# Field-pair products of six batches a chunk: summed by halving on GpSimd instead of by VectorE, gathers of a duo issued without a pause

## The reference

```python
e = jnp.stack([tbl_0[ids[:, 0]], ..., tbl_39[ids[:, 39]]], axis=1)     # (2048, 40, 64)
p = e[:, rowidx]
q = e[:, colidx]
z = jnp.einsum('bie,fie,bif->bi', p, param, q)                         # (2048, 780)
h = jnp.concatenate([z, dense_ctx], axis=1)
h = jnp.maximum(h @ W_top1 + b_top1, 0.0)                              # 512 wide
h = jnp.maximum(h @ W_top2 + b_top2, 0.0)                              # 256 wide
y = h @ W_top3
```

## Time and profile before

| | us |
|---|---|
| median of three runs | 1375.43 (1375.16 to 1380.41) |
| the profiled execution, its time | 1380.23 |
| its span, first to last instruction | 1378.2 |
| PE busy | 1242.5 |
| DVE busy | 1032.1 |
| POOL busy | 604.4 |
| ACT busy | 697.6 |

### The profile page before, as it was taken

The page is one execution under the profiler, slowest core; times in us unless marked ns, Lnnn a source line. Parts: engine busy times, 40 slices in busy tenths (PEclk is TensorE's granted clock), DMA queues, the critical chain, the costliest instruction groups (busy, mean ns, idle before and its releaser), DMA issues.

```text
span 1378.2 us, 20032 instructions
## 1 busy us (share of the span) xinstructions
PE 1242.5 (90%) x6032; PEld 435.1 (32%) x6032; DVE 1032.1 (75%) x899; ACT 697.6 (51%) x5257; POOL 604.4 (44%) x646
## 2 busy tenths in 40 slices
PE   0446799989899999999999999999999999999999
PEld 0112233233233333333333333333333333333333
DVE  0124687878887878888887878888887888888970
ACT  0013366475554366484555366485555366485441
POOL 4555555555555554555555555554454454000000
PEclk9777899999999999999999999999999999999999
DMA  3111122222222222222222222222222222111100
GB/s 124 26 34 43 49 66 57 65 57 62 60 64 59 65 58 64 57 70 60 58 65 60 63 58 65 58 71 57 56 64 65 53 59 62 41 52 47 47 10 0
DMA packets 50531, 77.55 MB, mean 56 GB/s; under 512 B 14004, under 2 KB 14260, under 8 KB 50296
## 3 DMA queue, kind: packets, MB, share of 16 engines
q1 hardware_dynamic: 29936, 55.26, 13.9%
q0 software_dynamic: 20480, 21.01, 7.9%
q10 hardware_dynamic: 8, 0.01, 0.0%
HBM read 76.22 MB, written 0.01 MB: 55 GB/s over the span
## 4 chain that ended last, share of the span: by engine, by line
PE 68%; DVE 3%; ACT 3%; issue 1%; another core or an unknown queue 0%; DMA 0%; POOL 0%; DVEq 0%
PE ring L476 28%; PE z_ps L495 14%; PE ring L482 12%; PE aux L414 5%; ACT act_prod L327 3%; DVE prod L400 2%; PE aux L446 2%; PE ring L414 2%; PE aux L421 2%; PE ring L477 1%; DVE sums L367 1%; PE aux L428 1%; PE ring L421 0%; DVE dve_prod L400 0%; PE aux L435 0%
## 5 line engine op out<-in xcount | busy, mean ns | idle before, releaser
L400 DVE TENSOR_TENSOR prod<-ring,emb 128x1024 f32<-128x1024 f32 x544 | 636.3, 1218 | 285.9 <-PE ring L477 264.0
L327 ACT ACTIVATE act_prod<-act_prod 128x64 f32<-128x64 f32 x2560 | 611.7, 242 | 144.0 <-DVE act_prod L400 110.6
L282 POOL DMA_INDIRECT stage<-tbl,idx x512 | 482.8, 943 | 450.5 <-issue 242.0
L476 PE MATMUL ring<-emb,raw 64*128 64x512 f32 x1088 | 570.9, 639 | 34.2 <-DVE prod L400 23.2
L477 PE MATMUL ring<-emb,raw 64*128 64x512 f32 x1088 | 571.9, 641 | 0.0
L327 ACT ACTIVATION_READ_ACCUMULATOR act_prod<-act_prod 128x1 f32 x2560 | 482.8, 189 | 2.3 <-issue 2.0
L476 PEld LDWEIGHTS ring<-emb,raw 64*128 64x128 f32 x1088 | 182.3, 192 | 376.9 <-issue 212.7
L495 PE MATMUL z_ps<-prod,sel 128*32 128x512 f32 x2176 | 262.4, 600 | 1.3 <-DVE prod L400 1.3
L482 PE MATMUL ring<-raw,emb 64*128 64x512 f32 x512 | 247.7, 614 | 4.1 <-DVE prod L400 3.1
L483 PE MATMUL ring<-raw,emb 64*128 64x512 f32 x512 | 247.8, 614 | 0.0
L294 ACT ACTIVATE emb<-aux 128x512 f32<-128x512 f32 x80 | 47.4, 592 | 316.4 <-PE aux L446 284.9
(11 more groups left out here) (32 smaller groups left out, 199.3 us busy)
## 6 DMA issues: line engine op xcount, KB each, us to landing
raw<-param_b SPq DMA_DIRECT2D x200, 256.0 KB
stage<-tbl,idx POOLq DMA_INDIRECT x512
kept<-tbl,idx POOLq DMA_INDIRECT x128
W<-W1g SPq DMA_DIRECT2D x1, 1792.0 KB
W<-W2t SPq DMA_DIRECT2D x1, 512.0 KB
idx<-ids_t SPq DMA_DIRECT2D x1, 240.0 KB, 3.6
z<-dense_t SPq DMA_DIRECT2D x4, 32.0 KB, 2.6
idx<-ids_t SPq DMA_DIRECT2D x1, 80.0 KB, 2.0
```

The source lines that it names most:

```text
L282: pool.indirect_dma_start(to[:, t, E * (f % 2) : E * (f % 2) + E], None, tables[f], bass.IndirectOffsetOnAxis(ap=idx[:, c, f, t : t + 1], ...
L327: op = act.activation(part, part, ACT.Copy, accum_out=sums[:, t, at : at + 1])
L400: dve.tensor_tensor(to, ring[:, n % RING, :, :], by, ALU.mult).then_inc(prod_done, 1)
L476: pe.matmul(ring[:, n % RING, 0, :], w[0:E], emb[0:E, PLACE[c, m], :], start=True, stop=True)
```

## The change

DVE no longer sums. Of the same six batches a chunk (now `POOL_SUMS`) POOL halves each unit's 16 runs of 64 five times (32, 16, 8, 4, 2 elements wide) in place and makes the last addition into `sums`: six additions for each unit, each waiting for the one before. These *folds* stand in POOL's program behind the eight gathers of a duo, at most two units behind one duo but for the last place; the table `POOL_AT` says where, by the rule that a unit's fold stands behind the gathers of duo n, the first for which duo n - 2 is turned later than that unit is made. The pause inside a duo is gone. Products for POOL have five places (before: three for DVE); `prod` shrinks from eight to seven, `y_out` becomes a part of `h1`. The first layer of the next chunk waits for the store of `y`, and in the tail ACT waits for the last such store ahead of the turn's copy instead of ahead of `y`.

```diff
-PROD = 2 * BATCH
-DPROD = 3
+PROD = 7
+PPROD = 5
-FLIGHT = 4
+LAG = 2
+FOLDS = 5
...
+POOL_AT = {}
+_order = sorted(DUO_AT)
+_place = 0
+for _c in range(NCH):
+    for _m in POOL_SUMS:
+        for _t in range(BATCH):
+            _u = NU * _c + BATCH * AT["samples", _m] + _t
+            while _place < NCH * DUOS and (
+                _place < LAG or DUO_AT[_order[_place - LAG]] <= _u or len(POOL_AT.get(_place, ())) == 2
+            ):
+                _place += 1
+            POOL_AT.setdefault(_place, []).append((_c, _m, _t))
...
+            def reduce(c, m, t):
+                if c and t == 0:
+                    pool.wait_ge(aux_ready, AUX_NO["turn", c - 1, (m - KEPT) // PER_GROUP] + 1)
+                pool.wait_ge(prod_done, NU * c + BATCH * AT["samples", m] + t + 1)
+                made = sampled(c, m, t)
+                part = pool_prod[:, made % PPROD, :, :].rearrange("p a (j e) -> p (a j) e", e=E)
+                half = E // 2
+                for fold in range(FOLDS):
+                    pool.tensor_tensor(
+                        part[:, :, :half], part[:, :, :half], part[:, :, half : 2 * half], ALU.add
+                    ).then_inc(pool_folded, 1)
+                    pool.wait_ge(pool_folded, FOLDS * made + fold + 1)
+                    half //= 2
+                pool.tensor_tensor(sums[:, t, sums_of(m)], part[:, :, 0], part[:, :, 1], ALU.add).then_inc(pool_reduced, 1)
...
                 for i, (f, t) in enumerate(product((2 * d, 2 * d + 1), range(BT))):
-                    if i == FLIGHT:
-                        pool.wait_ge(landed, 16 * (2 * BT * times + FLIGHT))
-                        pool.sem_inc(pool_waited, 1)
                     pool.indirect_dma_start(
...
+                for x in POOL_AT.get(n, ()):
+                    reduce(*x)
+            for x in POOL_AT.get(NCH * DUOS, ()):
+                reduce(*x)
...
-                if unreduced:
-                    reduce(*unreduced)
-                unreduced = (c, x, t) if kind == "samples" and x in DVE_SUMS else None
...
-                pe.wait_ge(dve_reduced, group_end(c, DVE_SUMS, g))
+                pe.wait_ge(pool_reduced, group_end(c, POOL_SUMS, g))
```

More of the change, by code:

```diff
@@ L43 @@
 NS = DUOS - KEPT
-DVE_SUMS = [KEPT + i for i in (1, 4, 7, 10, 13, 15)]
-ACT_SUMS = [m for m in range(KEPT, DUOS) if m not in DVE_SUMS]
+POOL_SUMS = [KEPT + i for i in (1, 4, 7, 10, 13, 15)]
+ACT_SUMS = [m for m in range(KEPT, DUOS) if m not in POOL_SUMS]
 BATCHES = []
@@ L107 @@
     AUX_AT.setdefault(NU * (_c + 1) + BATCH, []).append(("turn", _c, 1))
-    for _m, _x in zip(DVE_SUMS, [("h1", _c, 0), ("h1", _c, 1), ("h1", _c, 2), ("h1", _c, 3), ("h2", _c, 0), ("h2", _c, 1)]):
+    for _m, _x in zip(POOL_SUMS, [("h1", _c, 0), ("h1", _c, 1), ("h1", _c, 2), ("h1", _c, 3), ("h2", _c, 0), ("h2", _c, 1)]):
         AUX_AT.setdefault(NU * (_c + 1) + BATCH * (AT["samples", _m] + 1), []).append(_x)
@@ L157, in fm_mlp_kernel @@
         act_prod = sb("act_prod", [P, APROD, 2, CH])
-        dve_prod = sb("dve_prod", [P, DPROD, 2, CH])
+        pool_prod = sb("pool_prod", [P, PPROD, 2, CH])
         sums = sb("sums", [P, BT, NS * 2 * ROWS])
@@ L167, in fm_mlp_kernel @@
         h2 = sb("h2", [P, H2 // P, CH])
-        y_out = sb("y_out", [1, CH])
+        y_out = h1[0:1, 0, :]
         ring = ctx.enter_context(nc.psum_tensor("ring", [P, RING, 2, CH], F32))
@@ L186, in fm_mlp_kernel @@
         act_reduced = sem("act_reduced")
-        dve_reduced = sem("dve_reduced")
+        pool_folded = sem("pool_folded")
+        pool_reduced = sem("pool_reduced")
         group_summed = sem("group_summed")
@@ L209, in sampled @@
         def sampled(c, m, t):
-            by = DVE_SUMS if m in DVE_SUMS else ACT_SUMS
+            by = POOL_SUMS if m in POOL_SUMS else ACT_SUMS
             return BT * (len(by) * c + by.index(m)) + t
@@ L301, in save_aux @@
                         act.wait_ge(consts_loaded, 16 * 5)
+                    elif n == 0:
+                        act.wait_ge(stored, 16 * c)
                     act.activation(h1[:, n, :], aux[:], ACT.Relu, bias=b1[:, n : n + 1]).then_inc(aux_saved, 1)
@@ L305, in save_aux @@
                 else:
-                    if c:
-                        act.wait_ge(stored, 16 * c)
-                    act.activation(y_out[:], aux[0:1, :], ACT.Copy).then_inc(aux_saved, 1)
+                    act.activation(y_out, aux[0:1, :], ACT.Copy).then_inc(aux_saved, 1)
                     act.wait_ge(aux_saved, AUX_NO[kind, c, n] + 1)
-                    act.dma_start(out_v[c : c + 1, :], y_out[:]).then_inc(stored, 16)
+                    act.dma_start(out_v[c : c + 1, :], y_out).then_inc(stored, 16)
             def save_z(c, g):
@@ L344, in _ @@
             act.wait_ge(tail_ready, 1)
+            act.wait_ge(stored, 16 * last)
             act.activation(z[:, z_place(last, "samples", 1), :], aux[:], ACT.Copy).then_inc(tail_saved, 1)
@@ L354, in _ @@
             act.wait_ge(tail_ready, 1 + H1 // P + H2 // P + 1)
-            act.wait_ge(stored, 16 * last)
-            act.activation(y_out[:], aux[0:1, :], ACT.Copy).then_inc(tail_saved, 1)
+            act.activation(y_out, aux[0:1, :], ACT.Copy).then_inc(tail_saved, 1)
             act.wait_ge(tail_saved, 1 + H1 // P + H2 // P + 1)
-            act.dma_start(out_v[last : last + 1, :], y_out[:]).then_inc(stored, 16)
+            act.dma_start(out_v[last : last + 1, :], y_out).then_inc(stored, 16)
             act.wait_ge(stored, 16 * NCH)
@@ L362, in _ @@
         def _(dve):
[L363 to L370, removed]
             dve.memset(sel[:], 0.0).then_inc(sel_zero, 1)
@@ L375, in _ @@
             dve.memset(sel[E:P, 31:32], 1.0).then_inc(consts_made, 1)
-            unreduced = None
             for n in range(NCH * NU):
@@ L396, in _ @@
                     else:
-                        if made >= DPROD:
-                            dve.wait_ge(dve_reduced, made - DPROD + 1)
-                        to = dve_prod[:, made % DPROD, :, :]
+                        if made >= PPROD:
+                            dve.wait_ge(pool_reduced, made - PPROD + 1)
+                        to = pool_prod[:, made % PPROD, :, :]
                 dve.tensor_tensor(to, ring[:, n % RING, :, :], by, ALU.mult).then_inc(prod_done, 1)
-                if unreduced:
-                    reduce(*unreduced)
-                unreduced = (c, x, t) if kind == "samples" and x in DVE_SUMS else None
-                if unreduced and t == BT - 1:
-                    reduce(*unreduced)
-                    unreduced = None
         @block.tensor
```

## The result

The changed kernel took 1556.23 us (median of four runs, 1552.49 to 1556.95), the kernel before beside it 1377.33 (four runs, 1375.16 to 1380.41): ratio 1.129 [1.126, 1.132], 12.9% slower. The forecast had the sign, but with 1430 us and an upper end of 1475 it missed the size by 126 us.

What follows compares the result with a forecast made beforehand. It took PE's pace between turns as the bound. POOL's folds delay turns by 21.8 + 1.7 + 3.0 + 11.1 + 4.6 + 12.1 = +54.3 us; on 1380.2 that is 1434.5, less 4.8 gives 1430 us, range 1370 to 1475.

Steps and rivals of the forecast that it cites:

- The folds in POOL's queue: Added work on POOL: gathers wait behind folds and PE's turns wait for folds; +54.3 us in sum.
- turn 0 of chunk 0: PE's first turn, waiting for the folds of place 20: start at 289.7 us instead of 267.9, +21.8.
- to turn 1: Stretch from turn 0 to turn 1 of chunk 0: 157.2 us on POOL, before 155.5, +1.7.
- chunk 1, turn 0 / turn 1: Stretches ending at chunk 1's two turns: 160.4 us (+3.0) and 163.5 us (+11.1), set by POOL.
- chunk 2, turn 0 / turn 1: Stretches ending at chunk 2's two turns: 160.4 us (+4.6) and 163.5 us (+12.1), set by POOL.
- chunk 3, turn 0: Stretch ending at chunk 3's turn 0: POOL needs 150.4 of PE's 159.2 us, so no change.
- F: Price on POOL of one unit's six additions: 3.9 us, between bounds of 2.6 and 4.6; break-even at 2.6.
- the walk: Stepping along POOL's in-order queue of gathers and folds to each turn of PE that waits; +54.3 us in sum.
- The reductions: 96 reductions taken off DVE: hidden behind the layers in chunks 1 to 3 (0), 12 us in chunk 0.
- (b): Pause inside a duo removed from POOL: a duo takes 11.9 us instead of 13.9, 10.0 where folds follow.
- Rival 3: On POOL, eight gathers land later (up to 8 us a stretch) or start late (24), 1500 within reach; chance 0.13, slower.
- R: Rival in the experiments' expectations: folds on POOL cause the loss, by a port or waits, the missing pause is harmless.

Runs made afterwards that it cites:

- m_after: The changed kernel, unchanged, run again on a fifth chip, where the kernel before took 1360.37 us: 1432.49 us.
- g_nopause: The kernel before with only the pause inside a duo taken out, DVE still summing, on a third chip (before: 1377.91): 1538.04 us.
- m_pause_from_12: The kernel before without the pause in duos 0 to 11 of chunk 0 alone, on the fifth chip: 1335.98 us, ratio 0.981 to before.
- e3: The changed kernel with five of each unit's six additions left out (sums not the reference's), on the first follow-up chip (before: 1357.49): 1332.8 us.
- e1: The kernel before with only the pause inside a duo taken out, on the first follow-up chip (before: 1357.49): 1321.74 us.
- m_nopause: The kernel before with only the pause inside a duo taken out, on the fifth chip (before: 1360.37): 1324.78 us.
- e4: The changed kernel, first unit's folds between fourth and fifth gather, second's behind the eighth, old pause in duos without folds: 1516.51 us (before: 1357.49).

## Why the forecast had the sign and not the size

Two mechanisms make the loss, and each was shown by a run that has it alone: the folds by m_after, the missing pause by g_nopause. I forecast the first and left out the second.

**The folds in POOL's queue: right.** On the chip of group 5, where no report is late, the forecast meets the same program:

| us | forecast | measured (m_after) |
|---|---|---|
| turn 0 of chunk 0 | 289.7 | 290.8 |
| to turn 1 | 157.2 | 156.9 |
| chunk 1, turn 0 / turn 1 | 160.4 / 163.5 | 160.3 / 163.8 |
| chunk 2, turn 0 / turn 1 | 160.4 / 163.5 | 160.3 / 163.7 |
| chunk 3, turn 0 | 159.2 | 155.9 |
| time | 1430 | 1432.49 |

The steps hold singly too. The first gathers of duos 9, 10 and 11 in m_after's timeline of POOL:

```profile
113.25 0.94 POOL L310 DMA_INDIRECT stage<-tbl,idx  x1 [2.81 <-issue]
...
125.15 0.94 POOL L310 DMA_INDIRECT stage<-tbl,idx  x1 [2.23 <-issue]
...
142.63 0.95 POOL L310 DMA_INDIRECT stage<-tbl,idx  x1 [0.54 <-issue]
```

A duo without folds takes 11.9 us, as forecast, and duo 10, the first with folds, starts at 125.15 (forecast 123). With folds a duo takes 17.5 us, forecast 17.8. The six turns wait 39.3, 21.2, 4.4, 12.7, 4.4 and 12.5 us for POOL: long at the first and some 10 us at turn 1 of chunks 1 and 2, as written down. Agreement to 3 us has luck in it. F is 0.3 us smaller than forecast, which by the walk (12F to the first turn) alone would have brought turn 0 some 4 us sooner, and duo 10 starts 2 us late. With F = 3.6 the same walk gives 154.8, 159.2 and 161.1 us for stretches that measured 156.9, 160.3 and 163.8. F is also made up otherwise: 3.24 us of work and 0.3 of hand-over, where I had 2.7 and 1.2, so POOL was busy 915 us and not 860. The forecast is also set against a before of 1380, while this chip runs before in 1360: the loss here is 72 us, forecast 54. POOL's queue sets the changed kernel's time; before, which PE sets, is 20 us quicker there. Late reports are the likely reason. In the five stretches from turn 1 of chunk 0 to turn 0 of chunk 3 m_pause_from_12, on the chip of group 5, pauses as before does; they take 756 us there and 776 in before, where 16 of the 17 late products lie in them, 19 us in sum.

**The reductions: right.** Hidden in chunks 1 to 3, 11.0 us in chunk 0, shown by e3 against e1.

**Two slips in the sums.** I took the last start of the x8 rows for the start of a turn: turns stand at 580.5 and 1199.2, not 580.8 and 1199.6, which shifts 0.4 us from one stretch to the next. And 0.1 us more for F makes the sum 4 us longer, not 3. Neither bears on the result.

**The pause: the step that failed.** Under "What is removed", (b), I booked the missing pause as a pure gain, 11.9 us a duo instead of 13.9. POOL has that gain. I did not ask what else the pause did: with four gathers in a row few reports are late and by little (17 products by 21 us in before, none over 2.3 us); with eight the reports of PE and ACT are held until about the last landing, and 82 products are late by 178 us. DVE gets a finished unit late, PE then gets its ring place late, and in the changed kernel POOL gets its products late as well. On the chips of groups 3 and 5 the same edit is worth +160 us and -36 us (g_nopause, m_nopause). Rival 3 looked for late landings and late gathers, 8 us and 24 us a stretch; the gathers run 1.25 us apart to the end and land 2.2 us after the last one, as before. The late ones were other engines' reports. That it put 1500 within reach came nearest to the 1556, for a wrong reason.

**Why the parts don't add.** On a chip that holds reports, the folds with the pause cost 190 us, the missing pause without folds 160, both 176. Without the pause POOL's duo is shorter, and while DVE is held POOL has slack: it waits 263 us for products in the changed kernel and 139 in m_after. The same stretch cannot be lost to both. What bounds the changed kernel changes from turn to turn, so the waits of the turns for POOL fell from 94.5 us (m_after) to 72.9 although the kernel is 124 us slower.

**TensorE's clock.** Behind long waits the turns' transposes take 421 ns instead of 272, and the granted clock falls from 0.968 in before to 0.933. I left that out. Where no report is held it hardly matters: m_after has 0.936 and meets the walk. Where reports are held it is a part of the loss: in the six stretches PE's matmuls were busy for 950 us in the changed kernel and for 902 in m_after. The means over the span hide this; by stretch the clock is 0.92 to 0.96 against 0.92 to 0.98.

**DVE and POOL side by side.** That DVE slows down while POOL adds was part of R. It does not: a product of DVE takes 1218 ns in before, in the changed kernel and in m_after.

**Open.** What in the chip holds the reports and halts ACT, and why only on some chips: of five chips in these groups, two showed none and three did, as did the one of the first measurement. Each chip was seen in one group only, so the chip is not told apart from whatever else differed between groups. Where reports are held the trace also lacks many updates of semaphores, in the kernel before too: of the 800 updates by which PE reports a unit it records 658, in m_nopause all. Whether taking the trace has a part in the hold is not shown. A wait that only spaces gathers, without work, was not tried, nor a gap other than the folds of e4.

## What to carry to other kernels

A wait that looks like lost time in one engine's queue may be what keeps the others' semaphores prompt: before booking its removal as a gain, run the kernel with it out and nothing else changed, on more than one chip. When a profile shows an engine idle though its producer has ended, see which other engine is released at the same instant, and what transfer landed then. And price work moved to GpSimd by a walk along its queue to the point where another engine waits for it: that walk, from nearby rows alone, was right to a few us where nothing else disturbed it.

## What the runs showed of the hardware

- Rows of gathers without a gap hold back the semaphore reports of PE and ACT on some chips: 1538 against 1325 us for one program. A row of six costs 69 us against rows of four. With rows of four, parted by 3.6 us of folds or by a wait, 11 to 24 of 800 products are late, by 14 to 28 us in sum, with rows of three none.
- On the same chips ACT stops for up to 1.1 us between sums of one unit that have no wait between them, 89 us in the changed kernel.
- On GpSimd a dependent addition starts 0.08 us after the one before it ends, and costs 0.18 us and 2.1 ns an element. Short runs cost no more: 16 runs of 2 elements took 242 ns.
- Eight gathers do not land later than four: POOL goes on 2.2 us after the last in both (2.19 at 846.23). Only the very first duo took 3.99 us on the chip of the forecast, 2.44 on the one of group 5.
